# A graph network kernel whose gathered rows are scaled by factors read from PSUM, and whose second sweeps over edges become masked maxima

## What is computed

```
feat = (x @ W).reshape(n_nodes, H, D)                 # H = 8, D = 64
el = einsum('nhd,hd->nh', feat, attn_l); er = einsum('nhd,hd->nh', feat, attn_r)
e = leaky_relu(el[src] + er[dst], 0.2)
m = segment_max(e, dst)                               # the largest of each node's edges
ex = exp(e - m[dst])                                  # the softmax numerators
denom = segment_sum(ex, dst)
out = segment_sum((ex / denom[dst])[:, :, None] * feat[src], dst)
```

## Time and profile before

| | us |
|---|---|
| median of 3 runs | 3413.53 |
| lowest and highest | 3412.39, 3418.34 |
| the profiled execution, its own time | 3424.56 |
| the span in its trace | 3422.8 |

### The profile page before, as it was taken

How to read it: one execution, slowest core, us unless ns; L and a number is a source line. 1 busy time by engine, 2 the same in 40 slices (tenths; PEclk the granted TensorE clock), 3 DMA queues, 4 the chain that set the end, 5 groups by cost and what they waited for, 6 DMA issues and landing times.

```text
span 3422.8 us, 53700 instructions
## 1 busy us (share of the span) xinstructions
PE 2659.2 (78%) x19026; PEld 2005.0 (59%) x19026; DVE 2337.8 (68%) x3395; ACT 1240.5 (36%) x2962; POOL 1089.1 (32%) x1238
## 2 busy tenths in 40 slices
PE   3666675988989999779918777777777777884999
PEld 1666665544545555679916555555555555683888
DVE  7999997687223444677788777676677776523886
ACT  1777776010001111100016555555555554402443
POOL 3000000011101222100037777777777776002000
PEclk9999988999999999889959999999999999856999
DMA  4334334523457774212137777777777776160553
GB/s 128 155 155 170 159 155 171 187 93 108 146 172 252 251 259 142 97 40 55 51 101 196 199 200 200 198 201 197 198 203 204 200 199 186 64 173 19 165 166 111
DMA packets 306388, 541.15 MB, mean 158 GB/s; under 512 B 105166, under 2 KB 208352, under 8 KB 305744
## 3 DMA queue, kind: packets, MB, share of 16 engines
q1 hardware_dynamic: 236976, 312.43, 27.9%
q0 software_dynamic: 69152, 225.28, 23.9%
HBM read 423.69 MB, written 115.11 MB: 157 GB/s over the span
## 4 chain that ended last, share of the span: by engine, by line
PE 65%; DVE 19%; issue 7%; ACT 5%; POOL 2%; DMA 2%; SPq 0%; POOLq 0%; DVEq 0%; ACTq 0%
PE ps L1369 24%; PE ps L1178 13%; PE ps L1357 8%; PE ps L1318 8%; DVE a L523 6%; DVE a L519 3%; DVE a L726 3%; PE ps L1316 3%; ACT oht L1066 2%; PE ps L1095 2%; DVE a L520 2%; ACT oh L1068 2%; PE ps L1147 2%; PE ps L1206 1%; PE ps L1149 1%
## 5 line engine op out<-in xcount | busy, mean ns | idle before, releaser
L1466 POOL DMA_INDIRECT a<-t,srci x502 | 533.9, 1063 | 520.2 <-DVE a L763 333.3
L1369 PE MATMUL ps<-a,oh 128*128 128x260 f32 x2008 | 500.0, 394 | 216.0 <-ACT oh L1068 106.1
L1178 PE MATMUL ps<-a 128*128 128x512 f32 x1200 | 575.4, 611 | 15.0 <-DMA a<-at_d 14.0
L1369 PEld LDWEIGHTS ps<-a,oh 128*128 128x128 f32 x2008 | 366.8, 192 | 348.8 <-issue 160.9
L1066 ACT ACTIVATE oht<-iota,ndl 128x128 f32<-128x128 f32 x830 | 333.3, 402 | 500.6 <-PE ps L1369 460.6
L924 DVE TENSOR_TENSOR a<-a,exb 128x520 f32<-128x520 f32 x502 | 330.0, 699 | 191.9 <-DMA a<-t,srci 187.3
L1147 PE MATMUL ps<-a 128*128 128x200 bf16 x1568 | 332.2, 270 | 163.1 <-DVE a L519 65.6
L1369 PE MATMUL ps<-wts,oh 128*128 128x260 f32 x1312 | 328.8, 396 | 116.5 <-ACT oh L1068 75.9
L1466 POOL DMA_INDIRECT wts<-t,srci x328 | 348.6, 1063 | 99.9 <-issue 99.3
L1318 PE MATMUL ps<-tbl,a 128*128 128x200 bf16 (+1 forms) x4692 | 372.2, 218 | 6.2 <-issue 6.0
L1369 PEld LDWEIGHTS ps<-wts,oh 128*128 128x128 f32 x1312 | 239.5, 192 | 204.9 <-ACT oh L1068 104.2
(11 more groups left out here) (259 smaller groups left out, 3873.0 us busy)
## 6 DMA issues: line engine op xcount, KB each, us to landing
a<-at_d SPq DMA_DIRECT2D x60, 1280.0 KB, 6.1
at_d<-a SPq DMA_DIRECT2D x49, 800.0 KB, 3.3
mt_d<-a SPq DMA_DIRECT2D x49, 800.0 KB, 4.9
a<-mt_d SPq DMA_DIRECT2D x30, 1280.0 KB, 6.1
a<-ot_d SPq DMA_DIRECT2D x98, 320.0 KB, 3.0
a<-trlo_d SPq DMA_DIRECT2D x49, 512.0 KB
ot_d<-a SPq DMA_DIRECT2D x49, 320.0 KB, 5.5
a<-t,srci POOLq DMA_INDIRECT x502, 3.8
```

The costliest lines, as they stand in the source:

```text
L1178: m = e.matmul(acc[f].rearrange("p (x d) -> p x d", x=8), X[:, hi, P * f:P * (f + 1)], a, start=(hi == 0), stop=False, skip_group_check=True)
L1369: t = e.matmul(pbig[s % 3][:, 512 * u:512 * u + 260], oh[:, so, k, :], hrows[2 * r + k][:, 260 * u:260 * (u + 1)], start=(k == 0), stop=(k ...
L1466: e.indirect_dma_start(out=hrows[2 * r + k], out_offset=None, in_=t2, in_offset=bass.IndirectOffsetOnAxis(ap=srci[:, k, s:s + 1], axis=0)) ...
```

## The change

Three things are done.

- **Numerators in PSUM.** Every fourth step VectorE waits for the numerators of the next four steps (`ex_in`), copies them with one instruction (128 x 64) from `exb` in SBUF to `exps_ps`, which lies in bank 6 of PSUM, and waits for its own copy (`head_ex`). The multiplies read the factors from there. SyncE's loads wait for the copies rather than for TensorE, four steps at a time.
- **Masked maxima.** Two more scans in the last "neg" job make `firstm` (0 up to the first node boundary of the partition, hugely negative behind it) and `lastm` (the same from the right). The 16 second sweeps become 16 `scalar_tensor_tensor`: fv = max(mask + cin, fv), over the same 782 columns.
- The semaphore `head_ex` is new; `head_mm` no longer holds SyncE back.

```diff
+        exps_ps = bank(6)[:, 0:128].rearrange("p (q w) -> p q w", q=8)
+        firstm, lastm = a5[:, 0:J], a5[:, 896:896 + J]
...
                         e.tensor_reduce(acol[:, 1:2], negt[:, :], AX, ALU.min).then_inc(*V.inc("least"))
+                        e.tensor_tensor_scan(firstm, negh[:, :], negh[:, :], 0.0, ALU.add, ALU.min).then_inc(*V.inc())
+                        e.tensor_tensor_scan(lastm[:, ::-1], negt[:, ::-1], negt[:, ::-1], 0.0, ALU.add, ALU.min).then_inc(*V.inc("row ends"))
...
-                for h in range(H):
-                    sweep(fv, fv, negh, h, cin[:, 0, h:h + 1])
-                e.wait_ge(*V.last())
-                for h in range(H):
-                    sweep(fv, fv, negt, h, cin[:, 1, h:h + 1], True)
-                e.wait_ge(*V.last())
+                for m, w in ((firstm, 0), (lastm, 1)):
+                    for h in range(H):
+                        e.scalar_tensor_tensor(out=fv[:, :, h], in0=m, scalar=cin[:, w, h:h + 1], in1=fv[:, :, h],
+                                               op0=ALU.add, op1=ALU.max).then_inc(*V.inc())
+                    e.wait_ge(*V.last())
...
-                e.wait_ge(ex_in[s % 8], 16 * (s // 8 + 1))
+                if s % 4 == 0:
+                    n = min(4, NS - s)
+                    for i in range(n):
+                        e.wait_ge(ex_in[(s + i) % 8], 16 * (s // 8 + 1))
+                    e.tensor_copy(exps_ps[:, s % 8:s % 8 + n, :], exb[:, s % 8:s % 8 + n, :]).then_inc(head_ex, 1)
+                    e.wait_ge(head_ex, s // 4 + 1)
                 for k in range(2):
                     bv = hrows[2 * r + k].rearrange("p (h d) -> p h d", h=8)
-                    e.tensor_tensor(bv, bv, col(exb[:, s % 8, 8 * k:8 * k + 8], 65), ALU.mult).then_inc(head_mul, 1)
+                    e.tensor_tensor(bv, bv, col(exps_ps[:, s % 8, 8 * k:8 * k + 8], 65), ALU.mult).then_inc(head_mul, 1)
...
-                if s >= 8:
-                    e.wait_ge(head_mm, s - 7)
+                if s >= 8 and s % 4 == 0:
+                    e.wait_ge(head_ex, s // 4 - 1)
```

More of the change, by code:

```diff
@@ L356, in program @@
         pe_look, pe_carry = sem("pe_look"), sem("pe_carry")
-        head_oh, head_mm, head_add, head_mul = (sem(n) for n in ("head_oh", "head_mm", "head_add", "head_mul"))
+        head_oh, head_mm, head_add, head_mul, head_ex = (sem(n) for n in ("head_oh", "head_mm", "head_add", "head_mul", "head_ex"))
         act_elu, act_heads2 = sem("act_elu"), sem("act_heads2")
```

## The result

The changed kernel takes **3335.5 us**, the median of four runs (3331.8 to 3338.0), against 3413.0 for four runs of the kernel before (3412.3 to 3418.3): a ratio of 0.9769, with a 95% interval of 0.9752 to 0.9786. That is 77.4 us less; the forecast was 95.2 less. The two profiled executions differ by more, 3424.6 - 3333.8 = 90.7 us.

What follows compares the result with a forecast made beforehand. Bound taken: GpSimd's gather issue in the head loop, stretched by VectorE's two-SBUF multiplies. Terms -87.9 + 2.3 - 13.1 + 3.5 = -95.2 us from the median 3413.5 gave 3318.3 us; range 3305 to 3350, 8 in 10.

Steps and rivals of the forecast that it cites:

- rival A: Head loop: another limit just below, 2.55 to 2.68 us a step, time 3337 to 3390 (about 3358 at 2.60); chance 0.11.
- What bounds the kernel: Head loop: GpSimd issues gathers without pause, 1.36 us each; VectorE multiplies with two SBUF operands delay their issue.
- A's sign: Head loop, profile after: gathers at 1.0 us or more, or GpSimd waiting for TensorE with the ring full.
- The loop: Head loop: with factors in PSUM all 810 gathers take the 0.947 us floor, 0.108 less each, -87.9 us.
- B: Head loop: the edit does not free GpSimd, loop stays at 2.72 us a step, about 3406 us; chance 0.08.
- C: Head loop: slower, VectorE becomes the pace with PSUM multiplies of 1.19 us, 3.00 a step, about 3520 us; chance 0.08.
- The 104 copies: Head loop: SBUF to PSUM copies every four steps, about 0.3 us each on VectorE, hidden; gather delay 0, at worst 4 us.
- The start: Start of the head loop: the first copy waits for four loads instead of one, +2.3 us on the path.
- The new scans: First convolution, step 41: two mask scans on VectorE delay an already late TensorE, +3.5 us, 0 at best.
- The masked maxima: Second sweeps ahead of the head loop: 16 maxima at 0.94 us replace scans taking 28.1 us in all, -13.1 us.
- The bound from above: Masked maxima with operands 8 columns apart: at worst two cycles a column as in the scans, no gain.
- The difference carried over: Whole kernel: median 11.0 us below the profiled execution of the kernel before, assumed to hold after the change too.

Runs made afterwards that it cites:

- e13: Changed kernel with each step's first multiply reading factors from SBUF again and the adds one step later, quick chip: 3389.9 us, 0.9914 of the kernel before.
- e5: Changed kernel with the first of each step's two multiplies reading SBUF again, SBUF buffers released as late as before, late chip: 1.0005 of the kernel before.
- e6: Changed kernel with half of the edge loop's matmuls left out, quick chip: 3331.3 us, 0.9757 of the kernel before.
- e11: Changed kernel with VectorE's adds one step later, quick chip: 3334.1 us, 0.9763 of the kernel before.
- e12: Changed kernel with adds one step later, mask scans moved, first four steps' factors copied singly, backward maxima as two wide ones, quick chip: 3323.4 us, 0.9732.
- e4: Changed kernel with eight backward maxima reading and writing side by side, one forward maximum writing side by side, quick chip: 3327.3 us, one run.
- e8: Kernel before with the counts ScalarE and TensorE wait against in the window stage raised to at least 1, late chip: 3506.3 us, one run.

## Why the prediction was right, and where it was not

The time lies within the range, 17.2 us above the forecast. It does not lie in the band of 3305 to 3327 that went with the forecast's chance of 0.73: it is in the part up to 3350 that was there for rival A's near half, and neither A nor any other rival happened. The mechanism held; that the range held too owes something to room made for another reason, and to the chip. On a late chip the same prediction would have met no gain at all.

*What bounds the kernel* was right for the chip of the first comparison and, by the times and by e13, for the three quick chips: GpSimd's issue, stretched by VectorE's two-SBUF multiplies. e5 and e13 show the stretch following the SBUF reads, e13 also the time; e6 speaks against TensorE as the pace. I laid the gathers of the kernel before against VectorE once more, by what ran in a gather's first 0.94 us: 151 met only adds and took 0.94 to 0.96 us, 255 met only multiplies and took 1.16 on average and up to 1.47, the same reading as the prediction's 168 and 245 at 1.19. It was not a property of the kernel alone: on the late chips the same loop takes 2.89 us a step, by the waits in a ring through TensorE, and there neither kernel is quicker. That is near to rival A, and A's sign, GpSimd waiting for TensorE, is there; but A had transfers and leftover stretch in mind, and the chance of 0.11 stood for a limit between 2.55 and 2.68. No row of the kernel before on the first chip showed it. Why TensorE's products come late there is not settled: the clock was at its high level where one came 4.5 us late, the ends in its records are modelled, and neither e6 nor e11 met a late chip.

*The loop*: -87.9 predicted (0.108 times 810 is 87.5, unrounded 87.8), -88.0 measured, by the mechanism given (a mean gather of 0.947, "issue" as the only wait). Rivals B and C are out: the multiply stays at 0.69. The 104 copies cost nothing.

*The start*: +2.3 predicted, +2.1 measured. *The new scans*: +3.5 predicted, 3.1 to 3.5 measured; e12 moved them and TensorE's wait was 2.20 again.

*The masked maxima*: **the term that failed, by size.** -13.1 predicted, -3.3 measured: one every 1.55 us, not every 0.94 (1.61 long, not 1.03). The failing sentence is that the step costs nothing, taken from line 930. That row is an instruction with one input tensor and an output side by side; the maxima read a second tensor and their scores 32 bytes apart, and e4 puts the difference on the read. Whether line 930 went free for its single input or for something else was not tested. The bound from above, "no gain", was right to be kept.

*The difference carried over.* The profiled execution of before lay 11.0 us above the median, and I carried this over to the changed kernel. Its own profiled execution lies 1.7 below its median. The 17.2 us are therefore: 4.5 from the sum (9.8 of maxima, less some 5 that the stages ahead and behind and the start gave), 11.0 from the carried difference, and 1.7. If the 11 us sat in the stretch, they were part of what the change removes, and the sum should have been made for a typical execution, some 77 us instead of 88; then the loop's -87.9 against -88.0 is a match for this one execution. The table above and the means of 1.036 to 1.044 on the late chips fit this; but a short execution of the kernel before was not caught with a profile on a quick chip (e8 met a late one), so it is not shown. Other stages vary too: of the same code, the subtraction started at 1770.5 us in the profiled run of the changed kernel and at 1775.8 in e11.

## What to carry to other kernels

Where GpSimd issues gathers without a pause, look at what VectorE runs beside them: one operand in PSUM took every stretch away for 0.22 us of copying per four steps. Price a strided operand from a row with the same number of inputs and a like step, or measure it; and if a profiled execution is off its median, ask which term of the sum the difference sits in before carrying it over. A gain measured on one chip can be nothing on another whose loop is paced by other waits, so name the next limit and how near it is.

## What the chips showed that I had not expected

- Two chips of five ran the head loop at 2.89 us a step with either kernel, where the chip of the first comparison ran 2.72 and 2.50 and the three quick ones 2.50 with the factors in PSUM. Outside the loop their stages took the same times within some 5 us ahead of it and 4 to 10 us more behind it. The granted clock of the loop was 0.87 to 0.92 there, 0.99 to 1.00 on the others (e6 aside).
- In e6, with half the matmuls in the same stretch, TensorE's granted clock fell to a mean of 0.66, between its levels of 1.2 and 2.4 GHz (0.5 and 1), where it was 1.00 with all of them; a matmul then took 587 to 592 ns on average instead of 392. Half the work left TensorE busy 621 us instead of 696.
- A masked maximum whose read steps 32 bytes takes 1.61 us for 782 columns against 1.02 side by side, while a stepped write on top of it costs nothing more. ScalarE, reading side by side and writing 32 bytes apart, made one plane every 1.49 us.
